# Where VectorE's scans of a Mamba layer write their states, and when a ranking stage's output stores are awaited

## The reference, cut to what matters

```
# part 1: for each batch, 1024 channels e, 1024 time steps t, 16 states n
u     = silu(conv(in_proj(ctx)))
B, C  = rows of x_proj(u)                  # 16 each
delta = softplus(dt_proj(...))
state[n] = exp(delta*A[n]) * state[n] + (delta*u)*B[n]      # a scan over t
y     = sum over n of state[n]*C[n]  + D*u
x     = x + tanh(g) * y * silu(layernorm(x))
# part 2
xn    = layernorm(x);  scores = xn @ w_router;  top 128 rows of each batch
rows  -> attention, MLP, gate -> written back;  out = x + tanh(g2)*(...)
```

## Time and profile before

| | us |
|---|---|
| median of three runs | 2764.08 |
| the profiled execution's own time | 2760.83 |
| its span, first to last instruction | 2759.1 |
| project stage | 0 to 157 |
| scan stage, first half | 157 to 935 |
| ranking stage, first half | 935 to 1032 |
| layer stage, first half | 1032 to 1215 |
| scan stage, second half | 1215 to 2058 |
| ranking and layer stage, second half | 2058 to 2759 |

### The profile page before, as it was taken

How to read it: one execution, slowest core, us unless ns; L and a number is a source line. 1 busy time by engine, 2 the same in 40 slices (tenths; PEclk the granted TensorE clock), 3 DMA queues, 4 the chain that set the end, 5 groups by cost and what they waited for, 6 DMA issues and landing times. The chain is left out here.

```text
span 2759.1 us, 38288 instructions
## 1 busy us (share of the span) xinstructions
PE 2518.9 (91%) x13528; PEld 1845.1 (67%) x13528; DVE 1983.6 (72%) x2516; ACT 1617.6 (59%) x3482; POOL 1578.1 (57%) x882
## 2 busy tenths in 40 slices
PE   8969999999999549889899999999988799999998
PEld 3346666666666318556688888888754676488853
DVE  5779999999999766569999999999978535110000
ACT  4578888888888443377887788888752205100000
POOL 1269999999999510038898899889861000000000
PEclk9989999999999759999999999999998899999999
DMA  7732253432522497762352353353319740344442
GB/s 281 250 103 82 62 150 84 140 107 70 161 69 62 181 373 277 276 197 80 120 183 86 116 194 106 115 177 115 114 52 341 264 148 22 122 146 152 153 153 99
DMA packets 252624, 412.55 MB, mean 150 GB/s; under 512 B 50833, under 2 KB 134801, under 8 KB 249873
## 3 DMA queue, kind: packets, MB, share of 16 engines
q1 hardware_dynamic: 238928, 353.98, 39.9%
q10 hardware_dynamic: 12160, 51.39, 4.6%
q0 software_dynamic: 1344, 4.72, 0.5%
HBM read 325.09 MB, written 84.94 MB: 149 GB/s over the span
## 5 line engine op out<-in xcount | busy, mean ns | idle before, releaser
L763 POOL TENSOR_TENSOR s_x<-s_hp,k_bC 128x1024 f32<-128x1024 f32 x272 | 643.2, 2367 | 67.1 <-DVE s_hp L1297 66.5
L739 POOL TENSOR_TENSOR s_x<-s_du,k_bB 128x1024 f32<-128x1024 f32 x254 | 601.2, 2375 | 40.2 <-PE s_py L888 24.1
L888 PE MATMUL s_py<-k_ident,s_x 128*128 128x128 f32 x4096 | 519.0, 273 | 17.5 <-POOL s_x L763 16.9
L888 PEld LDWEIGHTS s_py<-k_ident,s_x 128*128 128x128 f32 x4096 | 462.5, 142 | 26.3 <-POOL s_x L763 21.2
L1222 ACT ACTIVATE s_pA<-s_delta,k_negA 128x512 f32<-128x512 f32 x512 | 333.9, 682 | 165.0 <-DVE s_x L1274 159.8
L1990 PE MATMUL l_p<-l_hT,l_ring 128*128 128x256 f32 x1792 | 390.3, 381 | 2.0 <-ACT l_hT L2095 1.4
L1990 PEld LDWEIGHTS l_p<-l_hT,l_ring 128*128 128x128 f32 x1792 | 342.3, 191 | 49.9 <-ACT l_hT L2095 1.6
L1222 ACT ACTIVATE s_x<-s_delta,k_negA 128x512 f32<-128x512 f32 x512 | 340.6, 710 | 0.0
L1100 ACT ACTIVATE s_xT<-s_duT,k_BT 128x128 f32<-128x128 f32 x1024 | 336.4, 389 | 0.1
L1297 DVE TENSOR_TENSOR_SCAN s_hp<-s_x,s_pA 128x512 f32<-128x512 f32 x256 | 309.7, 1212 | 32.0 <-ACT s_x L1222 18.0
L1297 DVE TENSOR_TENSOR_SCAN s_hp<-s_x,s_carry,s_pA 128x512 f32<-128x512 f32 x256 | 324.3, 1269 | 11.4 <-PE s_pA L870 4.4
(11 more groups left out here) (239 smaller groups left out, 3714.6 us busy)
## 6 DMA issues: line engine op xcount, KB each, us to landing
k_bC<-scratch_xd SPq DMA_DIRECT2D x32, 1024.0 KB, 11.7
scratch_ug<-p_ug ACTq DMA_DIRECT2D x16, 1024.0 KB, 4.3
k_u<-scratch_ug SPq DMA_DIRECT2D x64, 256.0 KB, 3.4
k_bB<-scratch_xd SPq DMA_DIRECT2D x32, 512.0 KB, 8.2
s_gy<-scratch_ug SPq DMA_DIRECT2D x64, 256.0 KB, 4.4
s_xt<-in_x SPq DMA_DIRECT2D x64, 256.0 KB, 4.7
scratch_x<-s_xt SPq DMA_DIRECT2D x64, 256.0 KB, 3.2
r_x<-scratch_x SPq DMA_DIRECT2D x32, 512.0 KB, 10.4
```

What stands on the lines that cost most here:

```text
L739: pool.tensor_tensor(out=x[:, 4 * g:4 * g + n], in0=du[:, s % 2:s % 2 + 1].broadcast_to([P, n, HALF]), in1=bB[:, into:into + n], op=ALU.mu ...
L763: pool.tensor_tensor(out=x[:, 2 * i:2 * i + 2], in0=hp_of(s, i), in1=bC[:, 2 * i:2 * i + 2], op=ALU.mult).then_inc(pool_hc, 1)
L888: last = nc.tensor.matmul(py[:, a], x[:, n, a * P:(a + 1) * P], ident[:], is_transpose=True, start=False, stop=n == NS - 1 and a == HALF / ...
```

## The change

In both scan stages, the scans of DVE's own pairs write their states to `x` in SBUF, over `added` (du times B), and DVE's product reads `x` and `bC`, both in SBUF, and writes `x` in place. `dA` stays in `pA`. So `pA` is free when the scans are done, and `release` waits for `scanned` for all pairs alike. The product now destroys the states, so in first halves it waits until ACT has copied their last column (`carried`), and stands one scan later in DVE's order. In the first half's ranking stage, 14 of the 16 tiles are kept in `bC` (8) and `bB` (6), and two in a tensor of its own; the stores of those 14 count on a semaphore that lives longer than the stage, and SP awaits them in the layer stage ahead of the loads of B and C.

```
 # Chosen
+        self.out_left = nc.alloc_semaphore(f"c{first}_out_left")
 # scan stage, PE, make_b
-                    before, pair = (s, i - 2) if i > 1 else (s - 1, i - 2 + NPAIR)
-                    if pair in vec_pairs(first, before):
-                        pe.wait_ge(vec_hc, after_vec(before, pair))
-                        if parts(before)[1] == 0:
-                            pe.wait_ge(carried, after_carry(before, pair))
-                    else:
-                        pe.wait_ge(scanned, NS * before + 2 * pair + 2)
+                    pe.wait_ge(scanned, NS * s + 2 * i - 2)
 # ACT, release
-                if i in vec_pairs(first, s):
-                    act.wait_ge(vec_hc, after_vec(s, i))
-                    if ends:
-                        j = 2 * (i % 2)
-                        nc.scalar.activation(kept, pA[:, j:j + 2, HALF - 1], ACT.Copy).then_inc(carried, 1)
-                        act.wait_ge(carried, after_carry(s, i))
-                else: ...
+                act.wait_ge(scanned, NS * s + 2 * i + 2)
+                if ends:
+                    states = hp_of(s, i) if i in pool_pairs(first, s) else x[:, 2 * i:2 * i + 2]
+                    nc.scalar.activation(kept, states[:, :, HALF - 1], ACT.Copy).then_inc(carried, 1)
 # DVE, times_C
-                j = 2 * (i % 2)
                 dve.wait_ge(scanned, NS * s + 2 * i + 2)
-                nc.vector.tensor_tensor(x[:, 2 * i:2 * i + 2], pA[:, j:j + 2], bC[:, 2 * i:2 * i + 2], ALU.mult).then_inc(vec_hc, 1)
+                if parts(s)[1] == 0:
+                    dve.wait_ge(carried, after_carry(s, i))
+                nc.vector.tensor_tensor(x[:, 2 * i:2 * i + 2], x[:, 2 * i:2 * i + 2], bC[:, 2 * i:2 * i + 2], ALU.mult).then_inc(vec_hc, 1)
 # DVE, scan
-                out = pA[:, n % 4]
+                out = x[:, n]
 # DVE, the loop
                     scan(s, 2 * i)
-                    times_C(s, i - 1)
+                    if parts(s)[1]:
+                        times_C(s, i - 1)
                     scan(s, 2 * i + 1)
+                    if not parts(s)[1]:
+                        times_C(s, i - 1)
 # ranking stage
-    x2 = sb("x2", [P, BUFS, DI])
+    late = first == 0
+    beside = []
+    if late:
+        for kept in (keep.bC, keep.bB):
+            flat = kept[:].rearrange("p n l -> p (n l)").rearrange("p (j d) -> p j d", d=DI)
+            beside += [flat[:, j] for j in range(kept.shape[1] * HALF // DI)]
+    OWN = BUFS - len(beside)
+    own = sb("x2", [P, OWN, DI])
+    x2 = [own[:, j] for j in range(OWN)] + beside
 # its SP stream, at the end
-            for j in range(BUFS):
-                sp.wait_ge(out_done[j], 16 * len(range(j, SPAN * TILES, BUFS)))
+            for j in range(OWN):
+                sp.wait_ge(out_done[j], 16)
 # its ACT stream
-                act.dma_start(t["out"][row(k):row(k) + P, :], x2[:, buf(k)[0]]).then_inc(out_done[buf(k)[0]], 16)
+                act.dma_start(t["out"][row(k):row(k) + P, :], x2[k]).then_inc(out_done[k] if k < OWN else chosen_rows.out_left, 16)
 # layer stage of the first half, SP
                 keep.load_delta(sp, t, SPAN, kept)
+                sp.wait_ge(chosen_rows.out_left, 16 * ((keep.bC.shape[1] + keep.bB.shape[1]) * HALF // DI))
                 for g in range(NS // 4):
                     keep.load_states(sp, t, SPAN, g, kept)
```

More of the change, by code:

```diff
@@ L1415, in route_stage @@
     p_pos = ctx.enter_context(nc.psum_tensor(f"r{first}_ppos", [P, 1], F32))
-    late = first == 0
     if not late:
@@ L1451, in load @@
             def load(k):
[L1452 to L1455, removed]
+                sp.dma_start(x2[k], t[f"x2_{first}"][k * P:(k + 1) * P, :]).then_inc(x_in[k], 16)
             def load_weights(j):
@@ L1574, in _ @@
                 j = buf(k)[0]
-                nc.scalar.activation(x2[:, j], x2[:, j], ACT.Identity, bias=offset[:, b, a:a + 1],
+                nc.scalar.activation(x2[j], x2[j], ACT.Identity, bias=offset[:, b, a:a + 1],
                                      scale=gain[:, b, a:a + 1]).then_inc(base_ready, 1)
@@ L1663, in take_stats @@
                 for h in range(H2):
-                    nc.vector.bn_stats(stats[:, k % 3, 6 * h:6 * h + 6], halves(x2[:, j], h)).then_inc(stats_done, 1)
+                    nc.vector.bn_stats(stats[:, k % 3, 6 * h:6 * h + 6], halves(x2[j], h)).then_inc(stats_done, 1)
             def mean(k):
@@ L1675, in score_tile @@
                     dve.wait_ge(scored, k - 1)
-                nc.vector.scalar_tensor_tensor(out=scrap[:, k % 2], in0=x2[:, buf(k)[0]], scalar=mv[:, b, a, 0:1], in1=router[:],
+                nc.vector.scalar_tensor_tensor(out=scrap[:, k % 2], in0=x2[buf(k)[0]], scalar=mv[:, b, a, 0:1], in1=router[:],
                                                op0=ALU.subtract, op1=ALU.mult, accum_out=raw[:, b, a:a + 1]).then_inc(scored, 1)
```

## The result

The changed kernel takes 2916.24 us (median of four runs, 2914.13 to 2917.56) against 2762.98 before (median of four runs now, where the three ahead of the prediction gave 2764.08). The ratio is 1.0554, 95% interval 1.0536 to 1.0572: slower by 153 us. The forecast was 2965, in a range from 2885 to 3080. Its profiled execution took 2915.03 us, 154 more than the one of before.

A forecast was written before the change was run, and what follows sets the result against it. POOL and DVE were taken to bound the first scan stage, DVE the second after the change. +111 + 94 - 4 = +201 us on 2760.8 gives 2962, with 3 us to the median 2965; range 2885 to 3080.

The forecast's parts named there:

- What bounds the scans: POOL (97%) and DVE (96%) set the first scan stage's length; in the second PE 97%, DVE 94%, POOL 88% busy.
- The product excludes POOL and POOL it: Scan stages: DVE's two-SBUF-input product and POOL's instructions block each other, costing POOL 1.08 us, DVE 1.10 or 1.00 per meeting.
- The bounds 0 and 2.37: Scan stages: DVE's wait when POOL is first lies between 0 and one whole POOL product, 2.37 us.
- First scan stage, +111: 112 products bring POOL to 877 us and DVE to 868; with 12 idle the stage takes 889, +111 us.
- Second scan stage, +94: 128 products bring POOL to 879 us and DVE, the bound, to 918; with 19 idle 937, +94 us.
- Early release, ceiling 22 and 24, taken in with the sums: Scan stages: ACT's waits of 95.6 and 72.1 us mostly go; gain at most 22 us (first), 24 us (second).
- Wait for the carry, taken at 0: First halves: the product waits for ACT's carry copy, bounds 0 and 60 us; taken as 0.
- Stores, -4: Ranking stage's end: stores awaited later let the layer stage start earlier, gain 0 to 6 us, taken as 4.
- Only POOL held up: Rival: in the scan stages DVE has priority and never waits, only POOL is delayed; 2910 us, chance 0.17.
- DVE waiting a whole instruction each time: Rival: in the scan stages DVE waits 2.37 us per product; 3240 us, chance of longer DVE waits (3060 to 3240) 0.11.
- A start effect: Within the rival of a faster kernel: POOL's 3383 ns at scan-stage starts came from a cold start, not exclusion.
- No gain as announced: Rival that the change does what it says: earlier release and stores give at most -50 us, likely 2735; faster, chance 0.07.

The follow-up runs named there:

- two experiments: Changed kernel with DVE's product between the two scans in all units: second input from pA in PSUM 2800.58 us, from bC in SBUF 2973.44 us.
- the ranking part alone: Kernel before, with only the ranking stage's tiles in bC and bB and their stores awaited in the layer stage: 2757.7 us, ratio 0.9984.
- the two half products: Changed kernel with each DVE product made as two 128x512 instructions, no wait between: 3210.04 us, ratio 1.1615.
- the kernel with one input: Changed kernel with DVE's product replaced by a multiply by 0.5 with one SBUF input and accumulated output: 2746.01 us, ratio 0.9948.
- the kernel with two pairs of four: Changed kernel with the scan part for pairs 0 and 4 only, pairs 2 and 6 as before: 2861.57 us, ratio 1.0364.
- the kernel with the second input from PSUM: Changed kernel, DVE's product multiplying by pA in PSUM, between the scans in all units, pA released after it: 2800.58 us, ratio 1.0137.

## Why the prediction was right, and by how much its steps were off

*What bounds the scans.* Right: POOL and DVE had 3 and 4% to spare in the first stage, and 181 us of added busy time there became 104 us of span.

*The product excludes POOL and POOL it.* Right, and shown on both sides. The hold on POOL of 1.08 us was taken from two start-up instructions; what the Trainium skill says ("SBUF — State Buffer", section "Who interferes with whom"), that whoever comes second is blocked, holds in both orders, for DVE up to 3.46 us where 1.19 is its own. The step that failed is the size of DVE's own wait: 1.10 us for a random arrival, 1.00 in the second stage. Measured are 1971 - 1199 = 0.77 and 1949 - 1199 = 0.75 us. Two things made it too large. DVE's arrival is not random: what is left of POOL's instruction when DVE comes is 0.87 us in the mean over the 240 products (nothing left counted as 0) and not 1.10. Of the 240, 54 took under 1.3 us, and many come at the same point of each unit: in the second-half units of the first scan stage 13 of the 16 products of pair 0 took 3.25 to 3.31 us. And the sum charged the whole rest, of which the last 0.12 us cost nothing. The bounds 0 and 2.37 were right. For POOL I took 1.08 a meeting; its busy time rose by 0.91 in the first stage and 0.82 in the second, because a DVE product that finds POOL idle or ends before it returns holds up nothing or less.

*First scan stage, +111.* Measured +104. POOL's busy time came to 857 and not 877, with 20 us idle and not 12, and DVE's to 825 and not 868.

*Second scan stage, +94.* Measured +53; this one term is most of the 49 us by which the forecast was high. DVE is the bound as said, at 879 of 898 us, with the 20 us of idle time I had left it. But it came to 879 and not 918, by 128 x 0.25 = 32 us of shorter waits and 7 us of shorter scans, those into `s_hp` too, of which I had counted about 3 and set the dearer product against them (it turned out no dearer: 1191 to 1200 ns where POOL was not in the way).

*Early release, ceiling 22 and 24, taken in with the sums.* It is worth about 12 us, the shorter scans and the later product with it, where the exclusion is absent. ACT's waits did not go away. The 95.6 us ahead of the exponentials are now mostly ahead of those of the odd pairs, and the copy of the carry waits 63.6 us for scans where it waited 72.1 for the product. Second scan stage of the changed kernel, total, times, longest:

```profile
ACT s_x L1211 <- DVE s_hp L1287: 92.9, 60, 3.0
ACT s_carry L1111 <- DVE s_x L1287: 63.6, 51, 3.2
...
ACT s_pA L1211 <- DVE s_x L1287: 14.7, 27, 1.0
```

ACT is ahead of DVE here, so where it waits matters little.

*Wait for the carry, taken at 0.* Right for the product one scan later; without that shift DVE stands idle for 52 us, as two experiments showed. My bound of 60 had been for the wrong place.

*Stores, -4.* Net -2 in the changed trace, -4 in the times of the ranking part alone.

*Rivals.* Only POOL held up: the time of 2910 is nearer to the 2916 than the forecast of 2965 is, but for a wrong reason, since DVE's products wait up to 2.27 us. The row cited for it did not test it: that router product began 0.17 us ahead of POOL's power. The next one came second, at 993.67, with 1.50 us of the power to go, and took 1.28 us against 1.23:

```profile
993.67 1.28 DVE L1676 SCALAR_TENSOR_TENSOR r_scrap<-r_x,r_mv,r_router 128x1024 f32<-128x1024 f32 x1
```

So a POOL instruction that reads 8 elements a partition hardly holds up DVE, where one of 512 or 1024 does. DVE waiting a whole instruction each time: no, but the two half products show that it happens where DVE comes twice in a row. A start effect: no. No gain as announced: the kernel with one input shows what the change would have given, 15 us.

## What to carry to other kernels

Before moving an operand from PSUM to SBUF on DVE, look at what POOL does meanwhile: a DVE instruction with two SBUF inputs and a POOL instruction that reads SBUF take turns, so each meeting costs POOL DVE's instruction and DVE what is left of POOL's, here 170 us over 240 products. (All of POOL's work that was stretched or in the way here reads 512 or 1024 elements a partition from SBUF.) Look for it in the profile as durations whose maximum is the sum of two instructions, not as idle time; and one stretched instruction at a stage's start can be the warning. If it can't be avoided, keep the instructions long: splitting each product in two cost 294 us more here.

## What the runs showed of the hardware

- The turn changes at the end of an instruction, also between two DVE instructions with nothing between: 2.84 us for 0.67 us of work. One product in the kernel with two pairs of four waited through four POOL instructions, 9.08 us.
- A DVE product that comes second takes 1.08 us from the end of POOL's instruction, 1.20 alone.
- A DVE multiply by a constant with an accumulated output, 128x1024 in SBUF, takes 1193 ns and did not stretch POOL's instructions (their means 2369 and 2377 ns, against 2367 and 2375 before the change).
- A scan of 128x512 from PSUM and SBUF takes some 10 to 15 ns less when it writes to SBUF: 1199 ns without and 1260 ns with a carry in the kernel with the second input from PSUM, against 1214 and 1269 before, in the same order of DVE's instructions. The order counts too: in the changed kernel's second scan stage the scans into `s_hp`, whose output did not move, went from 1212 to 1194 ns without a carry.
